# Convolution taps scaled on ScalarE and summed by accumulating DMAs, instead of scaled and summed on GpSimd

## The reference, cut to what matters

```python
qkv = x @ Wqkv;  q, k, v = split(qkv)
# 11 fixed offsets 0, 1, 2, 4, ..., 512: a softmax over k shifted by each offset
sc   = sum_d(q * k_shifted) / sqrt(d)      # one score for each token, offset and head
tele = sum over offsets of softmax(sc) * v_shifted
conv = causal depthwise convolution of v with 7 taps (conv_w: 128 channels x 7)
low  = linear attention with elu(.)+1 features
h = (tele + conv + low) @ Wo
```

## Time and profile before

| what | value |
|---|---|
| median of 3 runs | 341.38 us (341.34 to 342.54) |
| span of the profiled execution, first to last instruction | 339.5 us |
| PE, DVE busy | 261.4 us (77%), 275.6 us (81%) |
| ACT, POOL busy | 176.8 us (52%), 196.6 us (58%) |
| bytes moved by DMA | 21.89 MB |

### The profile page before, as it was taken

One profiled execution on the slowest core, in us unless ns is written; L12 is line 12 of the kernel. 1 busy time (PEld: TensorE's weight loads), 2 busy tenths in 40 slices (PEclk: granted clock), 3 DMA queues, 4 the chain that ended last, 5 costly groups with the idle time before them and its releaser, 6 DMA issues.

```text
span 339.5 us, 4554 instructions
## 1 busy us (share of the span) xinstructions
PE 261.4 (77%) x1527; PEld 175.7 (52%) x1527; DVE 275.6 (81%) x555; ACT 176.8 (52%) x443; POOL 196.6 (58%) x193
## 2 busy tenths in 40 slices
PE   6666667089379699997788499998795878888894
PEld 6323342087334537667455237767443277685374
DVE  5079866188999999989999999989999999845752
ACT  1683055302538755593569344775484606176852
POOL 4960999601889995306899980327979943131013
PEclk9785996569879959999999659999999559989999
DMA  7200376000025700200049300100248200000003
GB/s 219 71 0 16 106 196 147 24 0 3 9 90 143 215 26 8 69 26 3 37 130 229 111 12 2 31 2 8 84 124 215 83 12 31 0 2 0 2 2 93
DMA packets 20038, 21.89 MB, mean 64 GB/s; under 512 B 3289, under 2 KB 16434, under 8 KB 20014
## 3 DMA queue, kind: packets, MB, share of 16 engines
q1 hardware_dynamic: 20014, 21.59, 22.9%
HBM read 5.07 MB, written 2.10 MB: 21 GB/s over the span
## 4 chain that ended last, share of the span: by engine, by line
DVE 48%; PE 24%; ACT 9%; SPq 7%; DMA 6%; issue 4%; POOL 2%; POOLq 0%; DVEq 0%; ACTq 0%
DVE prods L263 12%; PE psH L1195 7%; DVE prods L880 6%; SPq L340 5%; DMA v_shift<-v_tok 5%; PE psA L1113 3%; DVE hid L994 3%; PE psY L1206 2%; PE psY L1292 2%; PE psA L1105 2%; DVE wgt L853 2%; PE psG L1278 2%; DVE gtmp L966 2%; SPq L339 2%; DVE gtmp L979 2%
## 5 line engine op out<-in xcount | busy, mean ns | idle before, releaser
L421 POOL TENSOR_SCALAR var<-ss 128x4 f32<-128x4 f32 (+1 forms) x25 | 13.4, 538 | 98.9 <-ACT squares L603 46.6
L263 DVE TENSOR_TENSOR prods<-qT,kT 128x1024 f32<-128x1024 f32 x32 | 55.4, 1778 | 12.4 <-ACT qT L530 12.4
L460 POOL TENSOR_TENSOR convT<-convT,tapT 128x1024 f32<-128x1024 f32 x24 | 57.9, 2412 | 2.0
L1195 PE MATMUL psH<-ident,prods 128*128 128x128 f32 x324 | 44.6, 290 | 0.0
L263 POOL TENSOR_TENSOR prods<-qT,kT 128x1024 f32<-128x1024 f32 (+1 forms) x12 | 28.8, 2418 | 23.2 <-PE psA L1163 11.3
L1195 PEld LDWEIGHTS psH<-ident,prods 128*128 128x128 f32 x324 | 40.5, 152 | 2.3 <-issue 2.3
L423 POOL TENSOR_TENSOR rstd<-var,neg_half 128x4 f32<-128x4 f32 (+2 forms) x29 | 37.8, 1305 | 2.4
L1163 PE MATMUL psA<-prods,slot_sel 128*32 128x512 f32 x168 | 26.0, 676 | 12.9 <-DVE prods L263 12.6
L880 DVE TENSOR_TENSOR prods<-v_shift,wgt 128x896 f32<-128x896 f32 x32 | 34.7, 1083 | 0.0
L880 DVE TENSOR_TENSOR prods<-v_tok,wgt 128x128 f32<-128x128 f32 (+2 forms) x60 | 25.8, 456 | 9.9 <-DMA v_shift<-v_tok 9.9
L1113 PE MATMUL psA<-xnT,wqkv 128*128 128x512 f32 x48 | 29.9, 767 | 5.0 <-ACT xnT L530 5.0
(11 more groups left out here) (194 smaller groups left out, 581.3 us busy)
## 6 DMA issues: line engine op xcount, KB each, us to landing
x_in<-L_attn_x SPq DMA_DIRECT2D x4, 512.0 KB, 4.0
x_res<-L_attn_x SPq DMA_DIRECT2D x4, 512.0 KB, 15.3
v_shift<-v_tok SPq DMA_DIRECT2D x4, 508.0 KB
v_shift<-v_tok SPq DMA_DIRECT2D x4, 504.0 KB
v_shift<-v_tok SPq DMA_DIRECT2D x4, 496.0 KB
v_shift<-v_tok SPq DMA_DIRECT2D x4, 480.0 KB
v_shift<-v_tok SPq DMA_DIRECT2D x4, 448.0 KB
out<-y_out SPq DMA_DIRECT2D x7, 256.0 KB, 2.3
```

The source lines that it names most:

```text
L263: return eng.tensor_tensor(prods[:, QUADS * (s % 2) + q, t0:T], qT[:, t0:T], kT[:, PRE - off + t0:PRE - off + T], ALU.mult)
L460: conv_chain(nc.gpsimd.tensor_tensor(convT[:], convT[:], tapT[:], ALU.add))
L1195: ins = pe.matmul(dst, terms[:, j % TERM_BUFS, m, :], ident[:], is_transpose=True, start=False, stop=(m == live[-1]))
```

## The change

POOL loses the three products and the whole arithmetic of the convolution. DVE makes all 11 products. ACT scales all seven taps (`scale_taps`), each as one [128 x 1024] activation with a per-channel scale, into five buffers: `convT`, `tapT`, and three tiles that are idle at that time (`qexp`, `xnT`, `kexp`); taps 5 and 6 reuse `tapT` and `kexp` once those have been added. POOL issues six DMAs for each batch (`sum_taps`) that add a source tile into a destination tile in SBUF (`accum_op`), each 128 partitions of 4096 bytes, 512 KB. Four of them add into `convT` and wait for one another; two add into `qexp`. New waits: ACT's fifth tap waits for the first sum, its sixth for the first even sum, ACT's copy of the next `xnT` for the second sum, its next features for all sums; DVE's `add_conv` waits for the fourth sum.

```diff
-POOL_PRODUCTS = ((1, 0), (1, 1), (2, 0))
+TAP_HOME = (0, 1, 2, 3, 4, 1, 4)
+N_SUMS, N_EVENS = 4, 2
-N_PRODUCTS = (4, 6, 8)
+N_PRODUCTS = (4, 8, 11)
+        def tap_buf(i):
+            return (convT, tapT, qexp, xnT, kexp)[i][:]
# POOL: products, conv_start, conv_taps are gone
+            def sum_taps(b):
+                def add(into, tap, added):
+                    nc.gpsimd.dma_start(tap_buf(into), tap_buf(TAP_HOME[tap]), accum_op=ALU.add).then_inc(added, N_DMA)
+                pool.wait_ge(tap_scaled, upto(b, TAPS, 2))
+                add(0, 1, sums_added)
+                pool.wait_ge(tap_scaled, upto(b, TAPS, 5))
+                add(2, 4, evens_added)
+                pool.wait_ge(sums_added, N_DMA * upto(b, N_SUMS, 1))
+                add(0, 3, sums_added)
+                pool.wait_ge(tap_scaled, upto(b, TAPS, 7))
+                pool.wait_ge(evens_added, N_DMA * upto(b, N_EVENS, 1))
+                add(2, 6, evens_added)
+                pool.wait_ge(sums_added, N_DMA * upto(b, N_SUMS, 2))
+                add(0, 5, sums_added)
+                pool.wait_ge(evens_added, N_DMA * upto(b, N_EVENS, 2))
+                pool.wait_ge(sums_added, N_DMA * upto(b, N_SUMS, 3))
+                add(0, 2, sums_added)
# ACT
             def evacuate_x(b):
+                if b:
+                    act.wait_ge(sums_added, N_DMA * upto(b - 1, N_SUMS, 2))
+            def scale_taps(b, shifts):
+                for shift in shifts:
...
+                    elif shift == 5:
+                        act.wait_ge(sums_added, N_DMA * upto(b, N_SUMS, 1))
+                    elif shift == 6:
+                        act.wait_ge(evens_added, N_DMA * upto(b, N_EVENS, 1))
+                    nc.scalar.activation(tap_buf(TAP_HOME[shift]), vT[:, VPRE - shift:VPRE - shift + T], ACT.Copy,
+                                         scale=cw[:, TAPS - 1 - shift:TAPS - shift]).then_inc(tap_scaled, 1)
             def features(b):
+                act.wait_ge(evens_added, N_DMA * upto(b, N_EVENS, 0))
+                act.wait_ge(sums_added, N_DMA * upto(b, N_SUMS, 0))
# order of ACT in round b
                     keep_normed(b)
+                    scale_taps(b, range(0, 5))
...
                         normalise1(b + 1, range(TPH if b else 0, NT))
+                    scale_taps(b, range(5, TAPS))
# DVE
-                mine = [q for q in range(QUADS) if TERMS[SLOTS * q + s] != LOW and (s, q) not in POOL_PRODUCTS]
+                mine = [q for q in range(QUADS) if TERMS[SLOTS * q + s] != LOW]
-                dve.wait_ge(conv_step, upto(b, N_CONV_STEPS, N_CONV_STEPS))
+                dve.wait_ge(sums_added, N_DMA * upto(b, N_SUMS, N_SUMS))
```

More of the change, by code:

```diff
@@ L61 @@
 PSA_AHEAD = 2 * 4
-N_PRODUCTS = (4, 6, 8)
+N_PRODUCTS = (4, 8, 11)
 N_SOFTMAX_STEPS = 5
-N_CONV_STEPS = 2 * TAPS - 1
 N_FRONT = 3
@@ L240, in block_kernel @@
         v_shifted, low_ready, low_used = sem("v_shifted"), sem("low_ready"), sem("low_used")
-        pool_prod_ready = sem("pool_prod_ready")
         terms_ready, terms_summed = sem("terms_ready"), sem("terms_summed")
-        conv_step, hT_ready, y_ready, yc_ready = sem("conv_step"), sem("hT_ready"), sem("y_ready"), sem("yc_ready")
+        tap_scaled, sums_added, evens_added = sem("tap_scaled"), sem("sums_added"), sem("evens_added")
+        hT_ready, y_ready, yc_ready = sem("hT_ready"), sem("y_ready"), sem("yc_ready")
         ss2_ready, x2_ready, ss3_ready, xn3_ready = sem("ss2_ready"), sem("x2_ready"), sem("ss3_ready"), sem("xn3_ready")
@@ L253, in block_kernel @@
         softmax_chain = Chain(softmax_step, N_SOFTMAX_STEPS)
-        conv_chain = Chain(conv_step, N_CONV_STEPS)
         def bank(tile):
             return tile // TPH, bass.ts(tile % TPH, P)
+        def tap_buf(i):
+            return (convT, tapT, qexp, xnT, kexp)[i][:]
         def product(eng, s, q):
@@ L492, in _ @@
             more_constants()
-            products(0, (1,))
             for b in range(B + 1):
@@ L500, in _ @@
                     ln4(u0 - 1)
-                if attn:
-                    products(b, (2,))
                 if more:
@@ L507, in _ @@
                 if attn:
-                    conv_start(b)
-                    conv_taps(b, range(1, TAPS))
-                    conv_chain.done()
+                    sum_taps(b)
                 if ffn and attn:
@@ L515, in _ @@
                     ln2(2 * b)
-                if more:
-                    products(b + 1, (1,))
                 if attn:
@@ L563, in evacuate_v @@
             def evacuate_v(b):
-                act.wait_ge(conv_step, upto(b, N_CONV_STEPS, 0))
                 for half in range(2):
                     evacuate(b - 1, PSA_V, half, vT[:, VPRE + half * HALF:VPRE + (half + 1) * HALF])
+            def scale_taps(b, shifts):
+                for shift in shifts:
+                    if shift == 0 and b == 0:
+                        act.wait_ge(conv_ld, 16)
+                    if shift == 0:
+                        act.wait_ge(hT_ready, upto(b, 2, 0))
+                    elif shift == 2:
+                        act.wait_ge(fq_ready, upto(b, 1, 1))
+                    elif shift == 4:
+                        act.wait_ge(fk_ready, upto(b, 1, 1))
+                    elif shift == 5:
[4 more added lines that the diff above has]
+                                         scale=cw[:, TAPS - 1 - shift:TAPS - shift]).then_inc(tap_scaled, 1)
             def features(b):
                 act.wait_ge(psA_free, freed(b - 1, PSA_Q, 1))
+                act.wait_ge(evens_added, N_DMA * upto(b, N_EVENS, 0))
                 nc.scalar.activation(kexp[:], kT[:, PRE:PRE + T], ACT.Exp)
                 nc.scalar.activation(fkT[:], kT[:, PRE:PRE + T], ACT.Relu).then_inc(k_feat, 1)
+                act.wait_ge(sums_added, N_DMA * upto(b, N_SUMS, 0))
                 nc.scalar.activation(qexp[:], qT[:], ACT.Exp)
@@ L1041, in _ @@
                 if attn:
-                    linear_state(b, gate_step_of(u0, 2 if more else 0))
+                    linear_state(b, gate_step_of(u0, 3 if more else 0))
                     if b == 0:
@@ L1045, in _ @@
                     if ffn:
-                        gates(u0, range(4 if more else 2, 24))
+                        gates(u0, range(5 if more else 2, 24))
                     softmax_logits(b)
@@ L1147, in sum_heads @@
                 pe.wait_ge(prod_ready, upto(b, N_PRODUCTS[2], N_PRODUCTS[s]))
-                if s:
-                    pe.wait_ge(pool_prod_ready, upto(b, len(POOL_PRODUCTS), s + 1))
                 if s == 2:
```

## The result

The changed kernel took 380.58 us in the median of 4 runs (376.64 to 385.68) against 341.36 us (341.22 to 342.54) for the kernel before. The ratio is 1.112, 95% interval 1.104 to 1.120; it is taken over the fast executions, and the one at 385.68 us counts as slow. The forecast was 385, range 353 to 424. The profiled execution has a span of 379.8 us, 40.3 us above the 339.5 us of before.

What follows compares the result with a forecast made beforehand. Bound: one DMA engine's backlog of shift copies. Rounds of +15.1, +11.9, +7.5 and +13.6 make +48, less 4 given back is +44 on 339.5, or 383.5, plus 1.9 around it 385 us; range 353 to 424.

Steps and rivals of the forecast that it cites:

- The bound before the change: Ahead of the weighing: the backlog of one DMA engine sets the shift copies' time, about 40.4 us from issue.
- DVE's relief is hidden: Between v_tok and the weighing: DVE perhaps 4 to 6 us earlier, limited by the copies' slack, 9.3 us in all.
- The sum by rounds: Delay of each round's weighing, less slack and first-multiplication gains: +15.1, +11.9, +7.5, +13.6, together +48 us.
- This term: Shift copies: six additions at two passes, 2.5 us each on the loaded engine, land them 15.1 us later each round.
- ACT's stand runs beside and is shorter: ACT at taps 5 and 6: exponentials some 6 to 7 us late, running beside the copies' delay without adding.
- the sign in all four rounds: DVE waits for v_shift in every round, 53 to 56 us from first shift copy to tile 0.
- Four us given back: Behind the weighing's start: PE and ACT finish expert work during the longer wait, 4 us back of L1292's 6.8.
- 3 for the first multiplications: Tile 0's first small multiplication in rounds 1 and 3, freed of POOL: 2 x 1.5 = 3 us gained.
- A: Rival on the lone engine: an addition costs one pass, 1.26 us; 359 to 366 us, chance 0.2.
- B: Rival at add_conv: the chain of additions is the bound; 449 us at 15 us an addition, chance 0.15.
- C: Rival: additions almost free beside the lone engine's traffic, DVE's relief wins; 329 to 339 us, chance 0.05.
- D: Rival: additions free, ACT's 6 us at taps 5 and 6 stay; within 0.5% up to +8, 341 to 350, chance 0.05.

Runs made afterwards that it cites:

- e3: The kernel before with the shift copies by 1 and by 4 tokens each split into two DMAs; 339.5 us, ratio 0.998 to the kernel before.
- e10: The kernel before with all eleven products on DVE, shift copies whole, convolution still on POOL; 337.9 us, ratio 0.992 to the kernel before.
- e6: The kernel before with all eleven products on DVE and the shift copies split, convolution still on POOL; 329.8 us, ratio 0.967 to the kernel before.
- e5: The changed kernel with shift copies by 1 and 4 tokens split and taps 5 and 6 in tiles of their own; 324.7 us, ratio 0.952 to the kernel before.
- e2: The changed kernel with taps 5 and 6 scaled into two further idle tiles (fkT and fk_tok), the DMAs the same; 378.0 us.
- e9: The changed kernel with additions cut to 16 of 1024 columns and taps 5 and 6 in tiles of their own; 339.5 us, ratio 0.997 to the kernel before.
- e1: The changed kernel with the shift copies by 1 and by 4 tokens each split into two DMAs; 335.4 us, ratio 0.986 to the kernel before.
- e8: As e5, with ACT's squares of the third norm moved ahead of the first five taps; 328.6 us, ratio 0.964 to the kernel before.
- e7: The changed kernel with POOL's six additions cut to 16 of 1024 columns, same count and waits; 356.7 us, ratio 1.049 to the kernel before.
- e4: The changed kernel with POOL's six DMAs a round as plain copies instead of additions; 375.9 us, ratio 1.103 to the kernel before.

## Why the prediction was right, and where it was not

- **The bound before the change**: right. The distance from the first shift copy to tile 0 is the quantity that moved, and the split shows that it was the load on few engines. What I missed is a second limit close behind in the kernel before, POOL's hand on DVE in round 0 (e3), so removing the backlog alone brings nothing there.
- **DVE's relief is hidden**: right, and larger than forecast. I had 4 to 6 us a round; DVE's busy time fell by 41 us, 10 a round. I had counted the products alone; they fell from 55.4 to 48.8 us, while three groups of small operations of the gates (`gtmp`) fell from 35.2 to 13.5. e10 shows it hidden (0.8%), e6 and e5 show it freed.
- **The sum by rounds**: forecast +15.1, +11.9, +7.5, +13.6 (rounds 1 and 3 with 1.5 off behind tile 0); measured +12.0, +11.7, +4.8, +12.9 ahead of tile 0. This term was too large: an addition delayed the copies of round 0 by 1.8 us (2.1 by e2 and e9), not 2.5, which is between one pass and two. With 1.8 the same sum would have been 10.8 of backlog in each round and 31 us before the 4 given back, and too low.
- **ACT's stand runs beside and is shorter**: this step failed. I priced the landing at 6 us and ACT's exponentials at 6 to 7 us late; the additions landed in 8.8 in the median, up to 13.8, and the exponentials of round 1 came 11.7 late. The first ones were issued while the shift copies and `x_res` kept all sixteen engines busy; with the split they land in 5.7 to 6.5 (e1). So in rounds 1 and 3 the last wait was ACT's, and the wait for `v_shift` that I named as the sign in all four rounds was there in round 0 and, barely, in round 2. e2 shows that the forecast limit stood directly behind it. Two errors of opposite sign, an addition too dear and a landing too early, met in the total. That the forecast of 385 came so near is in part luck.
- **Four us given back** behind tile 0, and 3 for the first multiplications: the stretches behind tile 0 gave back 1.0 in all. The two 1.7 us rows did go to 0.28, but nothing else followed.
- **Rivals**: A's price (one pass) is nearer to the 1.8 than the forecast's, but its time, 359 to 366, kept the early landing. B's wait of `add_conv` did not come in the changed kernel; it came, small, in round 0 of e1, e5 and e8, once the copies were split. C and D held the additions to be free, and the 52.4 us of round 0 against 41.6 in e7 exclude that. D's other half, ACT's stand by itself, is what e7 shows, and it costs twice the 8 us that D allowed: 356.7 against 339.5 us in e9.

## What to carry to other kernels

Before giving a stage to DMAs, find the busiest single DMA engine and what waits for it: a share of 0.06 over long stretches is one engine of sixteen at work, and cutting the copies so that they spread was worth more to the changed kernel (45 us) than all else, but nothing to the kernel before, where another limit stood beside it. A buffer that must be free before the next step can run makes an in-order engine wait for a landing, and the landing was set here by what was queued ahead more than by size: 8 KB took 2.0 to 9.9 us. When two limits end together, an experiment that removes one shows nothing; remove both before calling either harmless.

## What the runs showed of the hardware

- An accumulating DMA of 512 KB over 128 partitions landed in 4.4 to 6.5 us (medians by tile) in e1, where the shift copies of round 1 had ended before it was issued, and in 4.9 to 13.8 us beside them (changed kernel); the plain load of the same size took 4.0.
- A DMA of 8 KB from POOL landed in 2.0 to 9.9 us (e7): 2.0 in the median for the last of a round, 7.5 and 8.8 beside the shift copies.
- By its packets an accumulating DMA of 512 KB took 2.9 us of each engine and a plain copy 1.6 (e4); the shift copies beside them were delayed by 1.8 and 1.6 us for each.
- Beside POOL's additions and scaled copies, DVE's multiplications of 128 to 256 columns with both operands in SBUF took up to 2.8 us a pair instead of 0.6 (e3); POOL's issue of a DMA (0.85 us) left DVE's products at 1.17 us each in the mean.
